# Query blocks and raw queries of a fused attention and FFN kernel: made on VectorE by head masks and copies instead of DMA transfers, and the tile turns placed behind the state products

## What is computed

```python
def taylor_exp(x):
    x2 = (x[..., :, None] * x[..., None, :]).reshape(*x.shape[:-1], FEATURE_DIM * FEATURE_DIM) / R2
    ones = jnp.ones_like(x[..., :1])
    return jnp.concatenate([ones, x / RRD, x2 / RD], axis=-1)
...
    A_qk = jnp.einsum('bhnd,bhmd->bhnm', qf, kf)
    A_qk = jnp.tril(A_qk)
    y = jnp.einsum('bhnm,bhme->bhne', A_qk, v)
    rms = jax.lax.rsqrt(jnp.mean(y * y, axis=-1, keepdims=True) + RMS_EPS)
    y = y * rms * g_weight
    out = y @ Wo.T
...
    xn = _layernorm(x, axis=-1)
    x = x + _L0_attn_ref(xn, ...) + _L0_ffn_ref(xn, ...)
```

## Time and profile before

| | us |
|---|---|
| median of 3 runs | 776.98 |
| lowest and highest of them | 776.66, 779.71 |
| the profiled execution | 778.44 |
| span of its slowest core (core 2) | 776.8 |
| span of its quickest core (core 3) | 770.3 |

### The profile page before, as it was taken

One profiled execution on the slowest core, in us unless ns is written; L12 is line 12 of the kernel. 1 busy time (PEld: TensorE's weight loads), 2 busy tenths in 40 slices (PEclk: granted clock), 3 DMA queues, 4 the chain that ended last, 5 costly groups with the idle time before them and its releaser, 6 DMA issues.

```text
span 776.8 us, 11456 instructions; the slowest of 8 cores (770.3 to 776.8 us)
## 1 busy us (share of the span) xinstructions
PE 693.1 (89%) x3995; PEld 339.4 (44%) x4050; DVE 419.9 (54%) x651; ACT 252.8 (33%) x332; POOL 64.1 (8%) x99
## 2 busy tenths in 40 slices
PE   2767878786798888899999999999999999999998
PEld 1333544453354444344444444444444444444443
DVE  6665656667766557437674634633474455400554
ACT  3544756565768544213332333323100000000000
POOL 3001011102102100001000000110010000000000
PEclk9978989999999999899999999999999999999999
DMA  7975637446588654368857633451355577300765
GB/s 146 214 126 106 116 55 164 117 132 156 157 215 230 164 144 122 107 206 256 284 187 260 204 108 109 133 192 55 120 177 190 161 221 216 108 1 0 205 203 190
DMA packets 65414, 121.49 MB, mean 156 GB/s; under 512 B 22096, under 2 KB 28112, under 8 KB 65360
## 3 DMA queue, kind: packets, MB, share of 16 engines
q1 hardware_dynamic: 46752, 64.46, 28.6%
q0 software_dynamic: 18608, 56.30, 26.7%
HBM read 103.30 MB, written 16.78 MB: 155 GB/s over the span
## 4 chain that ended last, share of the span: by engine, by line
PE 83%; issue 5%; DVE 4%; DMA 4%; ACT 3%; SPq 1%; DVEq 0%; ACTq 0%
PE pST L1182 8%; PE pSS L1182 7%; PE pW L1182 7%; PE pY L1204 7%; PE pST L1204 7%; PE pW L1204 7%; PE pSS L1204 7%; PE pY L1182 7%; PE pW L1121 4%; PE pSS L964 4%; PE pW L964 3%; PE pSS L1121 3%; PE pSS L953 3%; DMA qf<-qkT 2%; PE pW L953 1%
## 5 line engine op out<-in xcount | busy, mean ns | idle before, releaser
L1204 PE MATMUL pW<-w2t,hT 128*128 128x512 bf16 x251 | 65.5, 379 | 0.3
L1204 PE MATMUL pY<-w2t,hT 128*128 128x512 bf16 x250 | 65.3, 379 | 0.4
L1204 PE MATMUL pST<-w2t,hT 128*128 128x512 bf16 x251 | 65.3, 380 | 0.3
L1204 PE MATMUL pSS<-w2t,hT 128*128 128x512 bf16 x251 | 65.3, 379 | 0.3
L1182 PE MATMUL pST<-xnT,w1t 128*128 128x512 bf16 x272 | 61.5, 379 | 0.0
L1182 PE MATMUL pSS<-xnT,w1t 128*128 128x512 bf16 x256 | 57.9, 379 | 0.4 <-DVE consts L687 0.4
L1182 PE MATMUL pW<-xnT,w1t 128*128 128x512 bf16 x256 | 57.9, 379 | 0.0
L1182 PE MATMUL pY<-xnT,w1t 128*128 128x512 bf16 x240 | 54.3, 379 | 0.0
L701 DVE TENSOR_SCALAR w1t<-stg,consts 128x2048 bf16<-128x2048 f32 (+1 forms) x18 | 21.0, 1166 | 55.2 <-PE pY L1182 55.0
L521 POOL DMA_DIRECT2D stg<-w1r x32 | 25.0, 781 | 262.8 <-DVE w1t L704 200.3
L701 DVE TENSOR_SCALAR w2t<-stg,consts 128x2048 bf16<-128x2048 f32 x16 | 20.5, 1283 | 43.2 <-PE pY L1182 26.6
(11 more groups left out here) (185 smaller groups left out, 1035.4 us busy)
## 6 DMA issues: line engine op xcount, KB each, us to landing
stg<-w1r POOLq DMA_DIRECT2D x32, 1024.0 KB, 7.0
stg<-w2r SPq DMA_DIRECT2D x16, 1024.0 KB, 8.4
stg<-w2r POOLq DMA_DIRECT2D x16, 1024.0 KB, 5.9
xr<-x SPq DMA_DIRECT2D x16, 512.0 KB, 5.6
res_scr<-rst SPq DMA_DIRECT2D x16, 512.0 KB, 6.5
res<-res_scr SPq DMA_DIRECT2D x32, 256.0 KB, 3.8
xs<-x SPq DMA_DIRECT2D x32, 256.0 KB, 4.4
out<-osb SPq DMA_DIRECT2D x32, 256.0 KB, 3.1
```

Of the source, the lines that this page charges most:

```text
L1204: return e.matmul(out_bank(n), hT[:, j, 128 * t:128 * t + 128], w2t[8 * dh + j // 4][:, j % 4, :], start=(j == 0), stop=(j == NJ - 1))
```

## The change

- The DMA transfers `q_block` and `q_raw` are gone from both queues, with their semaphores, the clearing of the second query block on GpSimd (one memset) and the places kept for them among the weight loads.
- VectorE makes them. Behind `empty_qk(B + 1)` it now runs `block_q(B + 1)`, 8 multiplications of 128x512 bf16 with a head's mask, and `raw_q(B + 1)`, two copies of 64x512 bf16, one for each half of the partitions. The first block gets `raw_q(0)` as well. Since a copy on VectorE stays on its partitions, the layout of `qf1`, `kf1`, `L1` and the mask `m1` is turned round: raw queries lie on rows 0 to 63 of group 0 and 64 to 127 of group 1, squares on the other half. The matmul L1031 has 96 rows of result instead of 64. Setting this up takes one instruction more in VectorE's first part and two more in its second.
- In TensorE's chunk, `y_before(i)` now stands ahead of the turned tile.

The core of the diff:

```diff
-            if side_unit(i) is not None and side_unit(i)[0] == "qk":
-                q_block(e, i // 4 + 1, range(4), dQS)
-                q_raw(i // 4 + 1)
...
-            if (kind, u) in Q_BEFORE:
-                q_block(e, Q_BEFORE[(kind, u)], range(4, 8), dQP)
...
+        def block_q(B):
+            q_ready(e, B)
+            for h in range(8):
+                e.tensor_scalar(qblk[:, B % 2, h, :], qkT[:, B % 2, 0, :],
+                                hmask[:, h:h + 1], None, ALU.mult).then_inc(dQM, 1)
+
+        def raw_q(B):
+            for g in range(2):
+                e.tensor_copy(qf1[64 * g:64 * g + 64, B % 2, g, :],
+                              qkT[64 * g:64 * g + 64, B % 2, 0, :]).then_inc(dQR, 1)
...
             if side_unit(i) is not None and side_unit(i)[0] == "qk":
                 empty_qk(B + 1)
+                block_q(B + 1)
+                raw_q(B + 1)
...
-                if B == 0:
-                    e.wait_ge(dQM, 8)
-                else:
-                    e.wait_ge(dQS, 64 * B)
-                    e.wait_ge(dQP, 64 * B)
+                e.wait_ge(dQM, 8 * (B + 1))
...
-                e.wait_ge(dQR, 32 * (B + 1))
+                e.wait_ge(dQR, 2 * (B + 1))
...
+            y_before(i)
             for t in turned_first(i):
                 turn_unit(t)
-            y_before(i)
```

More of the change, by code:

```diff
@@ L96, in square_unit @@
     return ("qv" if 2 <= B <= 4 else "qg", B)
-N_FIRST = 18
-N_SETUP = 27
+N_FIRST = 19
+N_SETUP = 30
 def unit_table():
@@ L150 @@
 ORD = [STG[:n + 1].count(STG[n]) for n in range(len(LOADS))]
-Q_BEFORE = {("a1", 2): 3, ("a1", 6): 4, ("a1", 9): 5, ("a1", 13): 6, ("t1", 1): 7}
 T_PE = 4
@@ L216, in build_program @@
     htmp = at("htmp", [128, 8], F32, 48.5)
-    hmask = at("hmask", [128, 8], F32, 48.75)
+    hmask = at("hmask", [128, 8], F32, 199.125)
     wo = at("wo_sb", [128, KD, D], BF16, 100)
@@ L233, in build_program @@
     L0 = at("L0", [128, 8, 8, 16], BF16, 194)
-    L1 = at("L1", [128, 8, 8], BF16, 196)
+    L1 = at("L1", [128, 3, 4, 8], BF16, 196)
     KX = at("KX", [128, 8, 64], BF16, 196.5)
@@ L241, in build_program @@
     mio = at("mio", [128, 2, 4], F32, 199.25)
-    mtmp = at("mtmp", [128, 4], F32, 199.5)
+    mtmp = at("mtmp", [128, 2, 4], F32, 199.5)
     m1 = at("m1", [128, 2, 4], F32, 199.75)
@@ L313, in build_program @@
     sA1 = S("sA1"); sA1D = S("sA1D"); sA2 = S("sA2"); aG = S("aG")
-    dQM = S("dQM"); dMK = S("dMK"); dW = S("dW"); dKF = S("dKF"); dRD = S("dRD"); dRC = S("dRC")
+    dQM = S("dQM"); dQR = S("dQR"); dMK = S("dMK"); dW = S("dW"); dKF = S("dKF"); dRD = S("dRD"); dRC = S("dRC")
     dNM = S("dNM"); dS1 = S("dS1"); sTR = S("sTR"); sTH = S("sTH"); sTC = S("sTC")
@@ L353, in values @@
         return v2[:, n - 16, :] if 16 <= n < 28 else vk[:, n % 2, 0:512]
-    def q_block(e, B, heads, done):
-        q_ready(e, B)
-        for h in heads:
-            e.dma_start(out=qblk[16 * h:16 * h + 16, B % 2, h, :],
-                        in_=qkT[16 * h:16 * h + 16, B % 2, 0, :]).then_inc(done, 16)
     def sync_stream(e):
@@ L380, in sync_stream @@
         e.dma_start(out=consts[:, C_B1:C_B1 + 32], in_=b1_d).then_inc(dC, 16)
-        def q_raw(B):
-            q_ready(e, B)
-            for g in range(2):
-                e.dma_start(out=qf1[64:128, B % 2, g, :],
-                            in_=qkT[64 * g:64 * g + 64, B % 2, 0, :]).then_inc(dQR, 16)
         def y_out(i):
@@ L400, in res_out @@
                                 in_=rst[:, c % 2, :]), c)
-        for t in range(3):
-            x_next(t)
-        e.wait_ge(sMS, 4)
-        q_raw(0)
-        for t in (3, 4):
+        for t in range(5):
             x_next(t)
@@ L494, in gp_stream @@
                         ).then_inc(dV1[n], 16)
-        q_block(e, 1, range(4, 8), dQP)
-        for n, i in enumerate((3, 4, 5, 7)):
-            if i == 7:
-                q_block(e, 2, range(4, 8), dQP)
+        for n, i in enumerate((3, 4, 5, 6)):
             slot(i)
@@ L578, in vec_stream @@
                             window, ALU.add))
-        pub(e.tensor_tensor(L1[:], Ix[:, :, 0:8], Ix[:, :, 8:16], ALU.add))
+        pub(e.tensor_tensor(L1[:, 2, :, :], Ix[:, 0:4, 0:8], Ix[:, 0:4, 8:16], ALU.add))
+        pub(e.tensor_tensor(
+            L1[:, 0:2, :, :],
+            Ix[:, 4:8, 0:8].unsqueeze(1).broadcast_to([128, 2, 4, 8]),
+            Ix[:, 4:8, 8:16].unsqueeze(1).broadcast_to([128, 2, 4, 8]), ALU.add))
         pub(e.tensor_copy(KX[:, :, 0:24], Ix[:, :, 0:24]))
@@ L645, in features_k @@
             e.tensor_tensor(
-                bass.AP(o1.tensor, o1.offset, [q1, [160, 2], [8, 4], [1, 8]]),
+                bass.AP(o1.tensor, o1.offset + 64, [q1, [64, 2], [8, 4], [1, 8]]),
                 bass.AP(k16.tensor, k16.offset, [p0, [256, 2], [64, 4], [1, 8]]),
@@ L727, in vec_stream @@
         empty_first("q", 0)
-        q_ready(e, 0)
-        for h in range(8):
-            e.tensor_scalar(qblk[:, 0, h, :], qkT[:, 0, 0, :], hmask[:, h:h + 1], None,
-                            ALU.mult).then_inc(dQM, 1)
+        block_q(0)
         empty_first("k", 1)
         ln_a(4)
-        e.wait_ge(sMS, 2)
+        e.wait_ge(sMS, 3)
+        raw_q(0)
         for i in range(NI):
@@ L875, in empty_side @@
             else:
-                e.activation(qf1[0:32, n % 2, 0, :], bank(key)[0:32, :], AF.Square)
-                ins = e.activation(qf1[32:64, n % 2, 1, :], bank(key)[32:64, :],
+                e.activation(qf1[64:96, n % 2, 0, :], bank(key)[64:96, :], AF.Square)
+                ins = e.activation(qf1[0:32, n % 2, 1, :], bank(key)[0:32, :],
                                    AF.Square)
@@ L1030, in side @@
                 q_ready(e, n)
-                mm = e.matmul(bank(key)[0:64, :], L1[:].rearrange("p h i -> p (h i)"),
+                mm = e.matmul(bank(key)[0:96, :],
+                              L1[:].rearrange("p g h i -> p (g h i)"),
                               qkT[:, n % 2, 0, :], start=True, stop=True)
```

40 lines of the change are left out of this document (20 added, 20 removed).

## The result

The changed kernel takes 792.86 us (median of 4 runs, 792.57 to 795.33) where the kernel before took 776.82 beside it: a ratio of 1.020, with a 95% interval from 1.017 to 1.022. It is slower, as forecast, but by 16 us and not by 7, and outside the range of 774 to 789. Executions in which one die ran at a visibly lower clock than the other are left out here and in all that follows.

A forecast was written before the change was run, and what follows sets the result against it. Bound: the attention loop, TensorE waiting for query transfers and VectorE's mask. Slow core: 776.8 - 4.2 - 0.7 - 2.3 + 0.35 + 10.8 + 0.2 + 2.5 = 783.4 us span; plus 1.6 around it, less 1: 784.0, range 774 to 789.

The forecast's parts named there:

- the main term: Late blocks 4 to 7: VectorE's new work delays the mask TensorE waits for, 10.8 us (8.8 to 12.0).
- The block: VectorE's new work for one query block: 2.8 us, between 2.3 and 3.1.
- The waits at blocks 4 to 7: TensorE's y_within waits longer for the mask: 2.8, 2.8, 2.5 and 2.7 us, together 10.8.
- The clock: Lower TensorE clock behind five longer gaps, blocks 3 to 7: 2.5 us in all, bounds 0 and 7.
- The turns: Own product starts 0.45 us sooner in chunks 1, 5, 6, 9 and 10: 2.3 us gained, range 1 to 4.
- Block 2 and block 1: Removed query transfers give back 4.2 us at block 2 on core 2 and 0.7 us at block 1.
- the start: At the kernel's start, raw_q(0) and the setup add about 0.2 us.
- In the early blocks there is slack: Early blocks: a turn and the own product between scores and y_within leave slack behind VectorE's new work.
- Block 3: The removed transfer's gain is lost again to a later VectorE: loss of 0.35 us on core 2, about 1.7 on quicker cores.
- Nothing gives it back: After blocks 4 to 7 the 10.8 us stay lost, since VectorE, ScalarE and TensorE are all shifted equally.
- the clock takes more: Rival: each gap gives back what chunk 31 shows, span 787.9 us, time about 788.5; chance 0.15.

The follow-up runs named there:

- the filled kernel: Changed kernel plus matmuls by a tile of zeros in TensorE's waits for the late mask (chunks 11, 15, 18, 22, 26): ratio 1.008 to before.
- the hybrid: Changed kernel with query blocks and raw queries of blocks 3 to 7 by transfer again: ratio 0.998 to before, median 777.73 us.

## Why the prediction was wrong in size

The mechanism of the main term was right: the mask late by the block, waits of TensorE for it in full at the late blocks, more than the removed transfers give. What failed is the size of the term for the clock, and the term for the turns. Point by point:

- **The block.** Forecast 2.8 us, measured 2.93: 2.11 for the multiplications (2.1 forecast), 0.63 for the copies (0.5), 0.19 for the wait (0.2). Right. (The Trainium skill, VectorE: DVE Perf Modes, the section on the TRN2 errata, gives by its formula an estimated 0.19 us for such a multiplication, and says itself that the formula comes out too low for a single operation. The trace has 0.264 and disagrees with the 0.19 again.)
- **The waits at blocks 4 to 7.** Forecast 10.8 us. In the filled kernel, where the clock is nearly out of it, the four stretches give 1.7 + 2.9 + 3.0 + 2.5 = 10.1, and block 4 had 0.9 us of its own slow clock filled away as well: 11.0. Right. Of the gaps themselves 5.6, 4.2 and three times 2.5 us were forecast and 5.75, 4.33, 2.75, 2.82 and 2.92 came. Mask waits of about 22 us in seven places were forecast; 24.4 in nine came.
- **The clock.** This is the first term that was mis-sized: 2.5 us, half a microsecond for each gap, with 7 as the upper bound. Filling took away 6.4 us on the mean, of which 0.9 was in the kernel before already, so the new waits cost about 5.5 us of clock on the mean, twice the forecast. On core 2 the stretches of blocks 3 to 7 hold 19.0 us, where 0.35 + 10.8 + 2.5 = 13.65 were forecast. The rows had shown that behind 3.69 us 2.9 are lost, and behind 2.86 about 1.1. I took less than half of the smaller of the two, for five gaps of about that length and more. The upper bound and the rival didn't follow from the rows either: five gaps at the 2.9 us of chunk 31 are 14.5, not 7, and would have made the rival's time 796, not 788.5. (The 2.9 is itself a little high, for the unit has 16 matmuls and one record is missing: from its start to that of the next unit it took 6.11 us there, and 3.45 in the changed kernel at the full level, so 2.7 were lost.)
- **The turns.** The second step that failed: 2.3 us, and a loss "isn't likely". In chunk 5 the distance from scores to own product is 2.75 us after and 2.79 before. The forecast let TensorE start when ScalarE's square ends. In neither kernel does it:

```profile
81.19 0.59 PE L1035 MATMUL pW<-qblk,qkT 128*128 128x512 bf16 x2
...
83.94 1.89 PE L953 MATMUL pW<-wv_sb,xnT 128*128 128x512 bf16 x8 [0.62 <-ACT Am L897]
```

```profile
82.36 1.12 ACT L897 ACTIVATE Am<-pW,consts 128x1024 bf16<-128x1024 f32 x1
```

  ScalarE ends at 83.48 and TensorE starts at 83.94, 0.46 us later. Before it was 84.71 and 85.22, 0.51 us later. The turn lay in that time and cost nothing; the swap only uncovered it. The same holds in chunks 6, 9 and 10, whose length changed by at most 0.2 us; chunk 1 alone gained, 0.7 us on the mean.
- **Block 2 and block 1.** Forecast -4.2 and -0.7 on core 2, with -2.3 for the turns and +0.2 for the start -7.0 at the scores of chunk 11; measured 136.73 - 141.38 = -4.65. The parts fit less well than the sum. At block 2 core 2 gains 3.7 us in chunks 7 and 8: the wait and the slow own product are gone, but `y_before` waits for ScalarE's signal here too:

```profile
110.67 0.38 PE L1059 MATMUL pY<-st,qf 128*128 128x256 bf16 x2 [1.46 <-ACT v L869]
...
111.67 1.89 PE L953 MATMUL pSS<-wv_sb,xnT 128*128 128x512 bf16 x8
```

  At block 1 core 2 loses 0.9 us in chunks 3 and 4 where 0.7 of gain was forecast. "In the early blocks there is slack" isn't borne out: chunk 3 is 1.1 us longer on every core, and chunk 7 0.8 us on core 3, which had no wait for a transfer there. The turns gave 1.0 us in chunk 1 and took 0.3 in the four others together. What evens the sum out is 1.7 us in chunk 2, for which the forecast has no term.
- **Block 3.** Forecast +0.35 on core 2 and +1.7 on a quick core. Filled: +1.3 on the mean; with the clock +2.7, and 22.11 - 19.64 = +2.5 on core 2. The wait that takes the transfer's place was foreseen; that its signal comes with the copy of the values was not, and is worth 0.45 us on core 2.
- **Nothing gives it back.** At chunk 31 core 2 got 2.7 us back: behind the same 3.69 us the output product took 3.61 us for 15 recorded matmuls, where it had taken 6.28. This is the clock again, by luck.

For core 2 alone the forecast was +6.7 us of span and the measurement +11.2: 2.35 up to chunk 11, block 3 2.1, blocks 4 to 7 with their clock 3.2 more, and 3.1 given back behind chunk 28. The rest of the 8.9 us between 784.0 and 792.86 is no step of the kernel: another core is the slowest, by 1.9 us (789.9 against 788.0), the time around the span is 2.7 us and not 1.6, and the median is 0.3 us above the profiled execution where I had put it 1.0 below. The cores were to come within 3 us; they are 5.5 apart, since the same waits cost some of them their clock and others not. The rival "the clock takes more" was the one that came true, and had 0.15; its own time, 788.5, is still 4 us short, for it kept the turns' 2.3 and priced the gaps too low.

## What to carry to other kernels

Work that is moved to an engine is to be placed behind what others wait for on it, not where its input becomes ready: the same 2.93 us a block cost 17.8 us in five stretches ahead of the mask and nothing (-0.7) behind it. A new wait of TensorE is to be priced at its length plus the slow matmuls that can follow it (here 2.75 us, and up to 2.5 more), and harmless matmuls in a wait that can't be removed buy the clock back; where there is no wait they cost their own time (3.0 us for 16 of them in chunk 30). When an instruction is moved into the shadow of another engine's result, the shadow ends only when the waiting engine starts, not when the other one ends.

## What the runs showed of the hardware

- After one and the same wait of 2.75 us, the output product took 5.94 us to the start of the next unit on core 2 and 3.45 on core 3. Behind 3.69 us in chunk 31 core 2 was slow in one kernel (6.28) and not in the other (3.61). The matmuls next to the two waits are the same; the level is not decided by the length of the wait alone.
- Sixteen products by zeros in the wait of chunk 31 kept the level: 3.40 us for 15 recorded matmuls. In the filled kernel the granted clock of core 2 rose from 0.87 to 0.95 and from 0.90 to 1.00 in two stretches, with VectorE as late as in the changed one.
- The wait for a transfer of raw queries was 3.13 us on core 2 before and 3.08 in the hybrid, whose TensorE came 8 us earlier (1.80 and 2.92 on core 3): an earlier arrival won nothing at a transfer that is itself issued only when the queries are there.
- Between the end of ScalarE's square and TensorE's start 0.46 to 0.51 us pass (chunk 5). Behind VectorE's mask, as its records end, it is less: the mask of block 6 ends at 240.68 + 0.68 = 241.36 and TensorE starts at 241.51.
